# Delta rule layer: key norms summed in the gaps of the last products, last query norm and square roots moved behind the first decays

## What is computed

```python
mixed = silu(causal depthwise conv of x @ W_qkv, 4 taps)      # q, k: 16 heads, v: 32 heads, all 128 wide
l2n = lambda t: t / jnp.maximum(jnp.linalg.norm(t, axis=-1, keepdims=True), 1e-12)
q, k = (l2n(q), l2n(k))                                        # each used by two value heads
A = -(einsum(k * beta, k) * decay) * strict                    # decay = exp(gc_i - gc_j), lower triangle
Tm = solve_triangular(eye - A, eye, lower=True)
# chunks of 64: v_new = Tm-products - state products; out = q-state product + (q k^T * decay) @ v_new
normed = core * rsqrt(mean(core * core) + 1e-6) * norm_w * silu(z)
y = einsum(normed, W_out)
```

## Time and profile before

| | |
|---|---|
| median of 3 runs | 2323.47 us (2316.97 to 2324.92) |
| profiled execution, its own time | 2323.68 us |
| its span, first to last instruction | 2321.7 us |
| PE busy | 1972.4 us (85%) |
| DVE busy | 1455.9 us (63%) |
| ACT busy | 843.4 us (36%) |
| phase c in the trace | roughly 740 to 1930 us |

### The profile page before, as it was taken

One profiled execution on the slowest core, in us unless ns is written; L12 is line 12 of the kernel. 1 busy time (PEld: TensorE's weight loads), 2 busy tenths in 40 slices (PEclk: granted clock), 3 DMA queues, 4 the chain that ended last, 5 costly groups with the idle time before them and its releaser, 6 DMA issues. The chain is left out here.

```text
span 2321.7 us, 26545 instructions
## 1 busy us (share of the span) xinstructions
PE 1972.4 (85%) x9860; PEld 1435.0 (62%) x9860; DVE 1455.9 (63%) x3232; ACT 843.4 (36%) x1348; POOL 157.3 (7%) x147
## 2 busy tenths in 40 slices
PE   6988987898995878998989999899998984777786
PEld 4868777554553557586675866757567572455464
DVE  3667665224222667867778676776767764767666
ACT  2434433111111544344443535444344421333243
POOL 2011010100002000000000000000000002012010
PEclk8989899899996889999999999999999996777786
DMA  3000000500002210202102021030210202000000
GB/s 133 6 14 10 6 5 5 192 0 10 0 0 89 39 37 13 53 19 46 38 15 51 28 37 38 15 70 10 37 38 20 45 1 73 8 12 15 7 5 5
DMA packets 132528, 72.14 MB, mean 31 GB/s; under 512 B 109808, under 2 KB 122672, under 8 KB 131408
## 3 DMA queue, kind: packets, MB, share of 16 engines
q1 hardware_dynamic: 132400, 70.44, 11.7%
HBM read 57.13 MB, written 13.11 MB: 30 GB/s over the span
## 5 line engine op out<-in xcount | busy, mean ns | idle before, releaser
L1286 PE MATMUL c_bank<-c_Y,c_NP 128*128 128x128 f32 x1536 | 179.5, 277 | 20.9 <-ACT c_Y L1439 20.9
L1286 PEld LDWEIGHTS c_bank<-c_Y,c_NP 128*128 128x128 f32 x1536 | 174.9, 192 | 26.5 <-issue 26.5
L1604 DVE TENSOR_TENSOR c_Y<-c_V,c_bank 128x512 f32<-128x512 f32 x192 | 131.8, 686 | 86.0 <-PE c_bank L1286 86.0
L1210 PE MATMUL c_bank<-c_xT,c_wqk 128*128 128x512 f32 x256 | 126.5, 641 | 3.7 <-ACT c_pad L1402 3.1
L1542 DVE SCALAR_TENSOR_TENSOR c_cv<-c_pad,c_wcqk,c_cv 128x1024 f32<-128x1024 f32 x96 | 122.2, 1279 | 9.5 <-ACT c_cv L1416 8.7
L1542 DVE SCALAR_TENSOR_TENSOR c_cv<-c_pad,c_wcv,c_cv 128x1024 f32<-128x1024 f32 x96 | 122.5, 1283 | 2.6
L1579 DVE SCALAR_TENSOR_TENSOR c_NP<-c_NP,c_cj,c_bank 128x256 f32<-128x256 f32 x256 | 104.8, 475 | 29.8 <-ACT c_NP L1445 29.8
L1362 PE MATMUL c_bank<-c_wout,c_yT 128*128 128x256 f32 x512 | 120.4, 381 | 0.0
L1278 PE MATMUL c_bank<-c_NP,c_Tb 128*128 128x256 f32 x512 | 116.0, 383 | 0.0
L1167 POOL TENSOR_TENSOR c_V<-c_Y 128x512 f32<-128x512 f32 x32 | 39.9, 1248 | 1115.4 <-ACT c_Y L1439 1115.4
L1210 PE MATMUL c_bank<-c_xT,c_wv 128*128 128x512 f32 x256 | 111.9, 595 | 3.6 <-DVE c_acc L1632 3.6
(11 more groups left out here) (406 smaller groups left out, 3942.2 us busy)
## 6 DMA issues: line engine op xcount, KB each, us to landing
b_wup<-b_in_wup SPq DMA_DIRECT2D x4, 1280.0 KB, 13.3
c_wqk<-c_in_wqk SPq DMA_DIRECT2D x9, 512.0 KB, 3.2
c_wv<-c_in_wv SPq DMA_DIRECT2D x8, 512.0 KB, 3.3
c_wz<-c_in_wz SPq DMA_DIRECT2D x8, 512.0 KB, 4.6
c_wout<-c_in_wout SPq DMA_DIRECT2D x8, 512.0 KB, 3.5
diagonal_blocks<-c_NP SPq DMA_DIRECT2D x64, 64.0 KB, 2.0
c_A<-diagonal_blocks SPq DMA_DIRECT2D x8, 512.0 KB, 3.7
c_NP<-no_blocks SPq DMA_DIRECT2D x32, 128.0 KB, 4.5
```

The source lines that it names most:

```text
L1210: last = pe.matmul(four(pair[q][:, :]), w[:, c * P:(c + 1) * P], xT[:, c, 4 * q:4 * q + 4, :], start=c == 0, stop=c == DC - 1)
L1286: last = pe.matmul(banks[n % 4][:, b * P:(b + 1) * P], lhsT(h, 4 * q + b), rhs(h, 4 * q + b), start=True, stop=True)
L1604: dve.tensor_tensor(rr(Y, h, q), rr(V, h, q), four(banks[n % 4][:, :]), ALU.subtract).then_inc(s["y_ready"], 1)
```

## The change

The sums of chunks 0 to 2 (both key norms and the first query norm) are made earlier on PE: chunk 2 between the fourth and the fifth group of the products C. DVE takes them out of PSUM by a maximum with 1e-24 into a new tile `sums`, and the factors `cj` come from the reciprocal of the sums, with no root. The sum of chunk 3 (the last query norm) is made behind the first three `decays_and_grams` and lies in bank 3. The root of all four is taken on ACT after five `decays` and after the root of the mean square; its reciprocal is made on DVE at the end of the round (`inverse_roots`). PE's last wait for `acc_step` moves to the fourth projection of the next round.

```diff
+        sums = sb("sums", [P, QK * B])
+        LAST_NORM = QK - 1
+        NORM_STEPS = KB + 3
+        def of_norms(k):
+            return nrm[:, k].rearrange("p k q b -> p (k q b)")
+        def norm_columns(m):
+            return banks[7][:, m * B:(m + 1) * B] if m < LAST_NORM else banks[3][:, D:D + B]
...
 PE, project:
+                if m == QK + 3 and r:
+                    pe.wait_ge(s["acc_step"], at(r - 1, B, B))
 PE, gram:
-                if u == 0:
-                    pe.wait_ge(s["root_ready"], at(i, 1, 1))
+                if u == 1:
+                    pe.wait_ge(s["sums_ready"], at(i, 2, 1))
 PE, round_:
                 for n in range(8):
+                    if more and n == 4:
+                        norms(i + 1, 2)
                     pe.wait_ge(s["y_ready"], at(i, 24, 16 + max(n + 1, min(n + 5, 8))))
...
+                if more:
+                    for n in range(AHEAD):
+                        decays_and_grams(i + 1, n)
                 pe.wait_ge(s["C_ready"], at(i, 8, 8))
                 if more:
-                    norms(i + 1, 2)
-                    norms(i + 1, 3)
-                    for n in range(AHEAD + 2):
+                    norms(i + 1, LAST_NORM)
+                    for n in range(AHEAD, AHEAD + 2):
                         decays_and_grams(i + 1, n)
...
-                pe.wait_ge(s["acc_step"], at(i, B, B))
 ACT:
             def take_root(r):
-                act.wait_ge(s["norms_ps"], at(r, QK, QK))
-                act.activation(root[...], banks[7][:, 0:QK * B], ACT.Sqrt).then_inc(s["root_ready"], 1)
+                act.wait_ge(s["sums_ready"], at(r, 2, 2))
+                act.activation(of_norms(0), sums[:, :], ACT.Sqrt).then_inc(s["root_ready"], 1)
...
                 if more:
-                    take_root(i + 1)
+                    for n in range(AHEAD + 2):
+                        decays(i + 1, n)
                 act.wait_ge(s["var_ready"], at(i, 2, 2))
                 act.activation(f[:, 1], f[:, 0], ACT.Sqrt).then_inc(s["rms_ready"], 1)
                 if more:
-                    for n in range(AHEAD + 2):
-                        decays(i + 1, n)
+                    take_root(i + 1)
 DVE:
             def factors(r):
+                early = LAST_NORM * B
+                dve.wait_ge(s["norms_ps"], at(r, QK, LAST_NORM))
+                dve.tensor_scalar(sums[:, 0:early], banks[7][:, 0:early], TINY * TINY, None, ALU.max)...
+                dve.wait_ge(s["sums_ready"], at(r, 2, 1))
+                dve.reciprocal(of_norms(2)[:, 0:early], sums[:, 0:early]).then_inc(s["norm_step"], 1)
+                ... (cj, two tensor_tensor, as before but not waiting for each other)
+            def last_norm(r):
+                late = slice(LAST_NORM * B, QK * B)
+                dve.wait_ge(s["norms_ps"], at(r, QK, QK))
+                dve.tensor_scalar(sums[:, late], norm_columns(LAST_NORM), TINY * TINY, None, ALU.max)...
+                dve.wait_ge(s["sums_ready"], at(r, 2, 2))
+                dve.reciprocal(of_norms(2)[:, late], sums[:, late]).then_inc(s["norm_step"], 1)
+            def inverse_roots(r):
+                dve.wait_ge(s["root_ready"], at(r, 1, 1))
+                dve.reciprocal(of_norms(1), of_norms(0)).then_inc(s["norm_step"], 1)
...
             def round_(i, more):
+                dve.wait_ge(s["norm_step"], at(i, NORM_STEPS, NORM_STEPS))
                 dve.tensor_copy(qinv[:, :, :, :], nrm[:, 1:3, :, 1, :]).then_inc(s["f_step"], 1)
...
+                if more:
+                    factors(i + 1)
                 dve.wait_ge(s["s2_ready"], at(i, 8, 8))
                 ... (f, the three steps up to var_ready)
                 if more:
-                    factors(i + 1)
+                    for n in range(AHEAD):
+                        decayed(i + 1, n)
+                    last_norm(i + 1)
                 dve.wait_ge(s["rms_ready"], at(i, 1, 1))
                 ... (f, reciprocal and scale)
-                if more:
-                    for n in range(AHEAD):
-                        decayed(i + 1, n)
                 for b in range(B):
                     ...
                 add_out(B - 2)
                 add_out(B - 1)
+                if more:
+                    inverse_roots(i + 1)
```

More of the change, by code:

```diff
@@ L996, in layer1_delta_rule @@
         sq = sb("sq", [P, 2, B, S])
-        root = sb("root", [P, KB, 2, B])
+        sums = sb("sums", [P, QK * B])
         nrm = sb("nrm", [P, 3, KB, 2, B])
@@ L1218, in norms @@
                 pe.wait_ge(s["sq_ready"], at(r, QK, m + 1))
+                into = norm_columns(m)
                 for b in range(B):
-                    last = pe.matmul(banks[7][:, m * B + b:m * B + b + 1], sq[:, m % 2, b, :], ones[:, :], start=True, stop=True)
+                    last = pe.matmul(into[:, b:b + 1], sq[:, m % 2, b, :], ones[:, :], start=True, stop=True)
                 last.then_inc(s["norms_ps"], 1)
@@ L1428, in take_root @@
             def take_root(r):
-                act.wait_ge(s["norms_ps"], at(r, QK, QK))
-                act.activation(root[:, :, :, :].rearrange("p k q b -> p (k q b)"), banks[7][:, 0:QK * B], ACT.Sqrt)\
-                    .then_inc(s["root_ready"], 1)
+                act.wait_ge(s["sums_ready"], at(r, 2, 2))
+                act.activation(of_norms(0), sums[:, :], ACT.Sqrt).then_inc(s["root_ready"], 1)
             def out_gate(i, b):
@@ L1496, in _ @@
                     silu(0, m - 1, first=True)
-            take_root(0)
             for n in range(8):
                 decays(0, n)
+            take_root(0)
             for i in range(0, ROUNDS - 1):
@@ L1558, in factors @@
             def factors(r):
-                link = Linked(dve, s["norm_step"], 3 + KB, r)
-                dve.wait_ge(s["root_ready"], at(r, 1, 1))
-                link(dve.tensor_scalar(nrm[:, 0], root[:, :, :, :], TINY, None, ALU.max))
-                link(dve.reciprocal(nrm[:, 1], nrm[:, 0]))
-                link(dve.tensor_tensor(nrm[:, 2], nrm[:, 1], nrm[:, 1], ALU.mult))
+                early = LAST_NORM * B
+                dve.wait_ge(s["norms_ps"], at(r, QK, LAST_NORM))
+                dve.tensor_scalar(sums[:, 0:early], banks[7][:, 0:early], TINY * TINY, None, ALU.max).then_inc(s["sums_ready"], 1)
+                dve.wait_ge(s["sums_ready"], at(r, 2, 1))
+                dve.reciprocal(of_norms(2)[:, 0:early], sums[:, 0:early]).then_inc(s["norm_step"], 1)
+                dve.wait_ge(s["norm_step"], at(r, NORM_STEPS, 1))
                 dve.wait_ge(s["gates_used"], r + 1)
                 for k in range(KB):
-                    link(dve.tensor_tensor(cj[:, 2 * k:2 * k + 2, :], betaR[:, 2 * k:2 * k + 2, :], spread(nrm[:, 2, k, 0, :], 2), ALU.mult))
-                link.close()
+                    dve.tensor_tensor(cj[:, 2 * k:2 * k + 2, :], betaR[:, 2 * k:2 * k + 2, :], spread(nrm[:, 2, k, 0, :], 2), ALU.mult)\
+                        .then_inc(s["norm_step"], 1)
+                dve.wait_ge(s["norm_step"], at(r, NORM_STEPS, 1 + KB))
+            def last_norm(r):
+                late = slice(LAST_NORM * B, QK * B)
+                dve.wait_ge(s["norms_ps"], at(r, QK, QK))
+                dve.tensor_scalar(sums[:, late], norm_columns(LAST_NORM), TINY * TINY, None, ALU.max).then_inc(s["sums_ready"], 1)
+                dve.wait_ge(s["sums_ready"], at(r, 2, 2))
[3 more added lines that the diff above has]
+                dve.reciprocal(of_norms(1), of_norms(0)).then_inc(s["norm_step"], 1)
             def decayed(r, n):
@@ L1651, in _ @@
             factors(0)
+            last_norm(0)
             for n in range(8):
                 decayed(0, n)
+            inverse_roots(0)
             for i in range(0, ROUNDS - 1):
```

2 lines of the change are left out of this document (1 added, 1 removed).

## The result

| | before | after |
|---|---|---|
| median of 20 runs | 2321.82 us (2315.71 to 2326.83) | 2326.12 us (2322.43 to 2335.67) |
| span of the profiled execution | 2321.7 us | 2324.7 us |
| ratio | | 1.0027, interval 1.0016 to 1.0038 |

The change makes the kernel 0.27% slower. I had forecast 2319.5 us, some 4 us less. The sign is wrong, and the next pages look for the term.

A forecast was written before the change was run, and what follows sets the result against it. At the round's start DVE's chain from `add_out` through elimination to two convolutions was taken as the bound. 1.94 us won less 0.39 and 0.95 for the clock, times seven boundaries, gave 4.2 us off 2323.68: 2319.5 us, range 2308 to 2330.

The forecast's parts named there:

- Part by part: Costing of the change at the first boundary at full clock: 1.94 less 0.39, net 1.55 us each, 10.9 us over seven.
- mark of the boundary at full clock: Boundary times after s, end of the sums of squares: `decayed(0)` within 1.6 us, `decayed(2)` 7.0, root load 8.3, `Y` 10.6.
- the gaps that it listed for PE: At the boundary, PE idle 908.7 to 910.8, 912.1 to 913.65, 918.0 to 919.2 and 920.1 to 922.3.
- The third norm between the C groups: Third norm sum between C groups 4 and 5: costs nothing, cover 0.6 us; without cover up to 1.84 us.
- The extra table load: Fourth ACT table load, before `decays(5)`: `decayed(4)` some 0.6 us later, hidden by PE's 0.96 us slack; without cover 0.6.
- The clock takes part of it back: Slow-clock stretches in the boundary's thinly filled new order: 0.95 us lost per boundary, leaving 4.2 us of gain over seven.
- bounds of 0 and 3.3: Clock loss per boundary: 0 if it never falls, at most 2.8 us on the path plus some 0.5.
- the dear fall: Slow stretch over `gcrow(3)`, gram 3, `gcrow(4)` and part of the last norm: 2.8 us, taken at one boundary in three.
- the cheap one: Slow stretch on the first loop steps: about 1 us, since PE also idles there; alternatively taken at most boundaries.
- Clock holds: Rival: full clock at nearly all boundaries, 10.9 us less, 2312.8 us; chance 0.27.
- Slower since the clock falls before the last norm and stays down: Rival: slow clock at each boundary through exponential 4, `Y` 2.8 us later, 0.5 lost in the loop, 2335.9 us; chance 0.08.
- The rival by ACT: Rival: table changes cost more than their row, up to the skill page's drain of 1.38 us, 2329 us; chance 0.04.

The follow-up runs named there:

- fill_dense: The changed kernel with eight dense products on PE behind gram 4, against the kernel before: ratio 1.0039, 2329.8 us.
- fill_all: The changed kernel with dense products (8, 5, 4 and 8) in PE's four waits at the boundary, against the kernel before: ratio 0.9969, 2313.59 us.
- exp_first: The changed kernel with a one-column exponential on ACT behind the norms' root, loading the table sooner, against the kernel before: ratio 1.0018, 2325.2 us.
- roots_sooner: The changed kernel with the reciprocal of the norms' roots ahead of the last two `add_out` on DVE, against the kernel before: ratio 1.0113, 2347.95 us.
- norm2_alone: The kernel before with only the third norm sum (chunk 2) moved between C groups 4 and 5: ratio 0.9905, 2298.37 us.
- last_norm_gap_2: The changed kernel with the last norm sum moved from behind gram 2 to between `gcrow(1)` and gram 1, against the kernel before: ratio 0.9968, 2316.26 us.
- norm2_fill: norm2_alone with seven dense products in PE's wait for the last copy of C, against the kernel before: ratio 0.9905, 2297.75 us.
- fill_thin: The changed kernel with eight one-column f32 products on PE behind gram 4, against the kernel before: ratio 1.0016, 2324.2 us.
- norm2_fill_both_2: norm2_fill with a wait for `z_ready` and seven and eleven dense products around the values' first transposes, against the kernel before: ratio 0.9826, 2280.57 us.

## Why the prediction was wrong

**Part by part.** Right. Every mark of the boundary at full clock is met within 0.2 us: the prediction's times against the first fence of the result. So are the gaps that it listed for PE, such as the last one, forecast from s + 9.5 to 11.7 and measured from 9.8 to 11.6. The third norm between the C groups costs nothing (65.30 us from products to s in both). The extra table load is hidden: with the clock held (fill_dense, fill_all) `Y` to copy is 25.85, 25.40 of before and the 0.45 of the reciprocal, and exp_first moved it for nothing. `inverse_roots` 0.45, forecast 0.39.

**"The clock takes part of it back".** This is the step that failed, by its size. I took 0.95 us a boundary between bounds of 0 and 3.3. Measured in the mean of the seven: `Y` to copy 27.58 - 25.85 = 1.73, and s to `Y` 11.41 - 10.44 = 0.97, together 2.7 us, nearer the upper bound. The sum becomes 2.10 won (12.54 - 10.44) less 0.45 less 2.7, a loss of 1.05 us a boundary and 7.4 in seven; the rounds show 7.5. I had named where a fall on the loop would lie, and priced it at "about 1 us, for there PE has idle time as well". It cost 1.73 and came at each boundary; the forecast counted the dear fall at one boundary in three or, for the same sum, the cheap one of 1 us at most of them, and never both at one boundary. Six of seven have both. The sentence behind it was the weak one: between ends far apart, and with gaps listed and one-column work among them, the nearest row was that of the earlier trace rows, where a gap and norm products stood before a fall. The kernel before has such a fall at every boundary. That speaks for the upper end.

**The rivals.** "Clock holds" is what fill_all makes of the change: 7 us below before (0.31%) where I had 10.9. "Slower since the clock falls before the last norm and stays down" happened once in seven in the traced execution; at five more the clock fell before the norm but rose again, for 0.6 us. It happened at six of seven in roots_sooner; I had it at 2.8 + 0.5 us, measured is 3.9 (14.38 against 10.44) for the part up to `Y`. The other slow way, a clock that falls in the loop at every boundary, was in none of my rivals, only in the forecast's bounds. The rival by ACT is refuted: exp_first moved the load and not the loop, and no drain shows beside a load.

**What I did not ask.** The forecast compared the whole change with the kernel before and nothing between. The part that wins is the third norm's place, 22 us by itself (norm2_alone). The rest, set on top, costs 28 us. In the traces, after has against norm2_alone 2.17 us more from s to `Y` (11.41 against 9.24) and 2.18 more from `Y` to copy (27.58 against 25.40). Of these 4.35 us a boundary the last norm behind gram 2 is 1.4 (last_norm_gap_2), the reciprocal 0.45, the fall in the loop 1.73, and the longer falls ahead of `Y` 0.64 (0.97 against 0.33), which leaves 0.1. The early decays, `decayed(0)` 2 to 3 us sooner, win nothing against that: before `Y` DVE waits 2.48 us for the fourth exponential (912.44) and 0.87 for ACT's root (915.28).

**What stays open.** Where exactly the clock falls in a given round I can't derive; I only see that dense fills move it, shorten it or remove it from a stretch. How the 3.3 us that norm2_alone wins at `Y` divide between the clock and the missing 1.84 us of products was not taken apart. The 20 times of after spread over 13 us, from 2322.4 to 2335.7; one trace of them can't say whether the slower ones have the long fall of the fourth boundary more often.

## What to carry to other kernels

Price each part of a change against the kernel without the others: one line of this one was worth 1%, and the other edits took it back and more. Where PE stands between waits with little, or with one-column, work, count the stretch behind it at half clock until a trace shows otherwise (in this kernel's loop such a stretch cost 1.73 us at each boundary), and look at what shares that stretch with the path. A few dense products that nobody reads, put into PE's waits, are a cheap test of this. Here they were also worth having (0.8% from the two that the last run adds), with the wait ahead of the last norm filled too. Filling a single stretch moved the fall into another and won nothing (fill_dense, norm2_fill), and one short fall a round is left in the fastest version.

## What the runs showed that I had not expected

Rounds repeat. In exp_first six rounds take 143.36 to 143.38 us each, in roots_sooner 146.77 to 146.84, with the fall in the same place each time; in fill_dense and fill_thin two patterns take turns (146.0 and 140.7; 143.7 to 143.8 and 142.9). An edit of 0.4 us changed the pattern, and with it each round by 3.4 us. So the time of a single small edit says little of its worth here: this one was to win 2.7 us and lost 22.

Dense products can cost less than nothing where PE waits: the 18 that norm2_fill_both_2 has more than norm2_fill in each round, some 4.2 us of work (1.67 and 2.54), made the round 2.4 us shorter.
